# Products for relative values over two tokens each, with near probabilities stored by pairs and four narrower transposes

## The reference

```python
B, T, C = x.shape                     # 8, 512, 128; H = 16 heads, d = 8
q, k, v = split(layernorm(x) @ w_attn)            # each (B, H, T, d)
rel = jnp.tril(idx[:, None] - idx[None, :])       # 0..511, clipped by indexing to 0..127
rk, rv = embk[rel], embv[rel]
att = jnp.einsum('bhtd,bhsd->bhts', q, k) * scale + jnp.einsum('bhtd,tsd->bhts', q, rk)
att = softmax(where(causal, att, -inf))
y = jnp.einsum('bhts,bhsd->bhtd', att, v) + jnp.einsum('bhts,tsd->bhtd', att, rv)
x = x + y.reshape(B, T, C) @ w_proj
x = x + experts(layernorm(x))
```

## Time and profile before

| | before |
|---|---|
| median of 3 runs | 797.58 us (796.44 to 797.76) |
| profiled execution, own time | 790.65 us |
| its span | 788.9 us |
| TensorE matmul busy | 705.4 us (89%) |
| VectorE busy | 588.3 us (75%) |
| ScalarE busy | 516.9 us (66%) |
| GpSimd busy | 255.8 us (32%) |

### The profile page before, as it was taken

The page is one execution under the profiler, slowest core; times in us unless marked ns, Lnnn a source line. Parts: engine busy times, 40 slices in busy tenths (PEclk is TensorE's granted clock), DMA queues, the critical chain, the costliest instruction groups (busy, mean ns, idle before and its releaser), DMA issues. The chain is left out here.

```text
span 788.9 us, 27137 instructions
## 1 busy us (share of the span) xinstructions
PE 705.4 (89%) x10368; PEld 511.1 (65%) x10368; DVE 588.3 (75%) x2036; ACT 516.9 (66%) x1032; POOL 255.8 (32%) x253
## 2 busy tenths in 40 slices
PE   3757779996989998988998988997999999999998
PEld 1545547775767677766777766775566666666665
DVE  6855667885878788888888878887367776776676
ACT  2576777885888777898887898877424434443331
POOL 9343355432545533445633535533000000000000
PEclk9897999998999999999999999999799999999999
DMA  9699999988688878778778678851000000000000
GB/s 305 230 277 287 329 271 291 299 268 253 220 250 264 292 229 249 239 217 268 232 230 253 211 239 252 260 160 47 2 22 27 27 1 27 28 15 0 14 15 14
DMA packets 116687, 140.32 MB, mean 178 GB/s; under 512 B 8848, under 2 KB 83088, under 8 KB 116368
## 3 DMA queue, kind: packets, MB, share of 16 engines
q1 hardware_dynamic: 116560, 138.59, 57.5%
HBM read 82.26 MB, written 56.30 MB: 176 GB/s over the span
## 5 line engine op out<-in xcount | busy, mean ns | idle before, releaser
L1041 DVE CUSTOM_DVE_ANT_0 ps<-ps,near 128x128 f32<-128x128 f32 (+3 forms) x512 | 244.8, 509 | 94.7 <-PE ps L812 63.1
L966 ACT ACTIVATE work<-ps,nmin 128x128 f32<-128x128 f32 (+3 forms) x512 | 249.8, 545 | 72.4 <-DVE nmin L1041 65.4
L824 PE MATMUL ps<-ident,work 128*128 128x128 f32 x1280 | 204.9, 280 | 13.9 <-issue 12.7
L824 PEld LDWEIGHTS ps<-ident,work 128*128 128x128 f32 x1280 | 159.0, 144 | 36.8 <-issue 18.9
L812 PE MATMUL ps<-kb,qb 128*128 128x128 bf16 (+3 forms) x512 | 131.5, 309 | 19.8 <-ACT work L966 15.9
L770 POOL TENSOR_SCALAR_AFFINE_SELECT work<-work 128x512 f32<-128x512 f32 x96 | 61.3, 638 | 242.2 <-ACT work L955 201.9
L1358 ACT ACTIVATE near<-ps 128x512 f32<-128x512 f32 x80 | 47.6, 595 | 136.6 <-PE ps L1323 136.5
L774 POOL TENSOR_TENSOR work<-work 128x512 f32<-128x512 f32 x96 | 124.3, 1295 | 8.0
L1026 DVE COPY work<-ps 128x512 f32<-128x512 f32 (+1 forms) x192 | 123.1, 641 | 1.0 <-PE ps L824 1.0
L1333 PEld LDWEIGHTS ps<-work,near 128*128 128x128 f32 x640 | 82.5, 191 | 34.3 <-issue 31.7
L841 PE MATMUL ps<-work,vb 128*9 128x128 f32 x2560 | 96.7, 279 | 0.8 <-ACT relS L944 0.8
(11 more groups left out here) (110 smaller groups left out, 629.6 us busy)
## 6 DMA issues: line engine op xcount, KB each, us to landing
near<-w_slots SPq DMA_DIRECT2D x96, 512.0 KB, 5.3
w_slots<-relS SPq DMA_DIRECT2D x128, 256.0 KB, 4.7
qk_rows<-work SPq DMA_DIRECT2D x36, 256.0 KB, 4.2
near<-w_slots SPq DMA_DIRECT2D x32, 256.0 KB, 4.6
w_slots<-near SPq DMA_DIRECT2D x8, 512.0 KB, 6.0
qk_rows<-y SPq DMA_DIRECT2D x9, 256.0 KB, 5.5
qb<-qk_rows SPq DMA_DIRECT2D x24, 96.0 KB
kb<-qk_rows SPq DMA_DIRECT2D x24, 96.0 KB
```

The costliest lines, as they stand in the source:

```text
L824: ins = nc.tensor.transpose(tp_ps[:, m % 2, n * P:(n + 1) * P], prob[:, m % PROBS, n * P:(n + 1) * P], ident[:, :])
L966: ins = nc.scalar.activation(prob[:, m % PROBS, h * wide:(h + 1) * wide], qk_ps[:, m % 3, h * wide:(h + 1) * wide], ACT.Exp, bias=nmin[:, ...
L1041: nc.vector.tensor_tensor_reduce(out=scores, in0=scores, in1=near[:, q % NEAR, a, 4 * P - wide:4 * P, r], scale=1.0, scalar=3e38, op0=ALU. ...
```

## The change

A product for relative values now covers two tokens, k and 64 + k. pcT is stored by pairs: for each k first the 32 heads of token k, then those of token 64 + k, so one product has 64 columns of weights. Its data are the 16 columns of both tokens in tv, which the host now orders by pairs. The output is 64 partitions x 16 columns, of which the two quarters that combine one token's probabilities with the other token's values are not used. The outputs of k = 0 to 31 lie at partitions 0 to 63 and those of k = 32 to 63 at partitions 64 to 127; the bank is filled over all its 512 columns. There are 64 products in an e, 8 in a chunk.

near_values(e, side) turns half of the bank with two transposes, each from 32 partitions of PSUM (one token of each pair) to the 32 partitions of rvn that hold these tokens. Side 0 runs where the single transpose ran, side 1 a slot later; for the last e both run in the same step. rvn_done now counts four for every e, and whoever waited for e + 1 waits for 4 (e + 1). GpSimd's instructions are the same in number, with the token dimension split in two.

```diff
@@ -553,7 +553,7 @@
         prob = prob.rearrange("p (n t) -> p n t", t=T)
         pT = pT.rearrange("p (k h t) -> p k h t", k=2, h=4)
         ptmp = ptmp.rearrange("p (h t) -> p h t", h=4)
-        pcT = pcT.rearrange("p (k t n) -> p k t n", k=2, t=P)
+        pcT = pcT.rearrange("p (k t n) -> p k t n", k=2, t=P // 2)
         rvn = rvn.rearrange("p (n d) -> p n d", d=D)
         ysum = ysum.rearrange("p (b h d) -> p b h d", b=2, d=D)
         yn = yn.rearrange("p (b c) -> p b c", b=GB)
@@ -609,7 +609,7 @@
         READ = {
             "rel": lambda q: (rel_done, q + 1),
             "av": lambda n: (av_copied, n + 1),
-            "rv": lambda e: (rvn_done, e + 1),
+            "rv": lambda e: (rvn_done, 4 * (e + 1)),
             "yt": lambda e, b: (ysum_done, GB * e + b + 1),
             "yb": lambda e: (ynT_done, e + 1),
             "pj": lambda e: (x1_done, e + 1),
@@ -761,9 +761,10 @@
                     wait_copied(pool, last(q))
                     if u == 0 and e >= 2:
                         pool.wait_ge(rv_ready, RVN * (e - 1))
-                    dst = pcT[:, e % 2, :, 4 * u:4 * u + 4].rearrange("p t h -> p h t")
+                    dst = pcT[:, e % 2, :, :].rearrange("p k (j n) -> p n j k", j=2)[:, 4 * u:4 * u + 4]
+                    by_pair = lambda v: v.rearrange("p h (j k) -> p h j k", j=2)
                     if i == 0:
-                        nc.gpsimd.tensor_copy(dst, pT[:, q % 2, :, 0:P]).then_inc(pc_done, 1)
+                        nc.gpsimd.tensor_copy(dst, by_pair(pT[:, q % 2, :, 0:P])).then_inc(pc_done, 1)
                         return
                     near_q = sum(row(k) > 0 for k in range(q))
                     wait(pool, pc_done, q)
@@ -771,7 +772,7 @@
                                             compare_op=ALU.is_gt, fill=0.0, base=0, pattern=[[0, 4], [-1, P]],
                                             channel_multiplier=1).then_inc(ptmp_done, 1)
                     pool.wait_ge(ptmp_done, near_q + 1)
-                    nc.gpsimd.tensor_tensor(dst, ptmp[:, :, :], pT[:, q % 2, :, i * P:(i + 1) * P],
+                    nc.gpsimd.tensor_tensor(dst, by_pair(ptmp[:, :, :]), by_pair(pT[:, q % 2, :, i * P:(i + 1) * P]),
                                             ALU.add).then_inc(pc_done, 1)
 
                 first["pool"](pool)
@@ -852,10 +853,10 @@
                     bank = misc("rv", e)
                     lot = 32 // RVN
                     for a in range(lot * c, lot * (c + 1)):
-                        for tq in range(4):
-                            tau = 32 * tq + a
-                            ins = nc.tensor.matmul(bank[32 * tq:32 * tq + NH, a * D:(a + 1) * D], pcT[:, e % 2, tau, :],
-                                                   tv[:, tau, :], start=True, stop=True)
+                        for side in range(2):
+                            k = 32 * side + a
+                            ins = nc.tensor.matmul(bank[64 * side:64 * side + 2 * NH, a * 2 * D:(a + 1) * 2 * D],
+                                                   pcT[:, e % 2, k, :], tv[:, 2 * k:2 * k + 2, :], start=True, stop=True)
                     ins.then_inc(rv_ready, 1)
 
                 def yt(e, b):
@@ -1042,20 +1043,24 @@
                                                        scale=1.0, scalar=3e38, op0=ALU.add, op1=ALU.min,
                                                        accum_out=nmin[:, k % MINS:k % MINS + 1]).then_inc(min_done, 1)
 
-                def near_values(e):
+                def near_values(e, side):
                     dve.wait_ge(rv_ready, RVN * (e + 1))
                     wait(dve, ysum_done, GB * e)
                     if e == 0:
                         dve.wait_ge(*first["third_rows"])
-                    nc.vector.transpose(rvn[:, :, :].rearrange("p n d -> p d n"),
-                                        misc("rv", e)[:, 0:32 * D].rearrange("p (t d) -> p d t", d=D)).then_inc(rvn_done, 1)
+                    for j in range(2):
+                        lot = slice(64 * side + 32 * j, 64 * side + 32 * j + 32)
+                        tokens = slice(64 * j + 32 * side, 64 * j + 32 * side + 32)
+                        nc.vector.transpose(rvn[tokens, :, :].rearrange("p n d -> p d n"),
+                                            misc("rv", e)[lot, :].rearrange("p (t j d) -> p j d t", j=2, d=D)[:, j]
+                                            ).then_inc(rvn_done, 1)
 
                 def normalise(e, b):
                     n = GB * e + b
                     dve.wait_ge(yt_ready, n + 1)
                     turned = misc("yt", e, b).rearrange("p (u q r) -> p u q r", u=4, r=32)
                     nc.vector.reciprocal(rden[:, b, :, :], turned[:, :, :, D]).then_inc(rden_done, 1)
-                    dve.wait_ge(rvn_done, e + 1)
+                    dve.wait_ge(rvn_done, 4 * (e + 1))
                     nc.vector.tensor_tensor(ysum[:, b, :, :].rearrange("p (u q) d -> p u q d", u=4),
                                             turned[:, :, :, 0:D],
                                             rvn[:, H * b:H * (b + 1), :].rearrange("p (u q) d -> p u q d", u=4),
@@ -1083,9 +1088,12 @@
                         pT_copy(m - 4)
                     if m < NU:
                         scores_min(m)
+                    for kind, *what in OPS[m - 2] if m > 1 else []:
+                        if kind == "rv" and what[1] == RVN - 1:
+                            near_values(what[0], 1)
                     for kind, *what in OPS[m - 1] if m else []:
                         if kind == "rv" and what[1] == RVN - 1:
-                            near_values(what[0])
+                            near_values(what[0], 0)
                         if kind == "yt":
                             normalise(*what)
                         if kind == "pj":
@@ -1096,7 +1104,8 @@
                 def last_row(step):
 
                     if step == 1:
-                        near_values(GI - 1)
+                        near_values(GI - 1, 0)
+                        near_values(GI - 1, 1)
                     if step in (2, 3):
                         normalise(GI - 1, step - 2)
                     if step == 6:
@@ -1466,7 +1475,8 @@
     heads = [4 * u + 2 * side + j for side in range(2) for u in range(H // 4) for j in range(2)]
     by_dim = np.arange(C).reshape(H, D)[heads].T.reshape(C)
     columns = np.concatenate([by_dim, C + by_dim, 2 * C + np.arange(C)])
-    turn = (np.arange(NREL)[None, :] - np.arange(P)[:, None]) % NREL
+    token = np.arange(P).reshape(2, P // 2).T.reshape(P)
+    turn = (token[None, :] - np.arange(P)[:, None]) % NREL
     def twice(rows):
         placed = np.zeros((P, rows.shape[1]), np.float32)
         for at, first_row, n in sum(PLACES, []):
```

## The result

| | kernel before | changed kernel |
|---|---|---|
| median | 797.53 us | 847.47 us |
| lowest and highest of 4 | 796.44, 797.76 | 844.38, 850.88 |
| profiled execution | 790.65 us, span 788.9 | 848.96 us, span 847.2 |
| mean granted clock | 0.970 | 0.931 |

Forecast was 833.9 us, range 808 to 852: direction and range hold, and the loss is 50 us where the sum said 36.3.

A forecast was written before the change was run, and what follows sets the result against it. TensorE was taken to set the pace, with VectorE following. Terms 25.3 + 1.4 + 15 + 2.6 - 3 - 5 = +36.3 us on a median of 797.58 gave 833.9 us, range 808 to 852.

The forecast's parts named there:

- The product's length: Line 857 on TensorE: loading 64 columns instead of 32 adds 0.21 us a chunk, +25.3 us over 120 chunks.
- Rival 4: TensorE's products: a record costs a fixed time whatever its columns, so the kernel gets faster, -8.3 us, 789.3; chance 0.06.
- rival 3: TensorE's products: two groups of 64 load as fast as four of 32 did, +9.4 us, 807.0; chance 0.06.
- The switch of width: TensorE from line 841 to 857: groups of 32 then 64 columns cost 0.11 us at 12 chunks, +1.4 us.
- Record stalls: Two unexplained mid-chunk stalls on TensorE, 4.1 us together, may be spared by half the records: -3 us.
- Absorbed: Until 190 us transfers limit, so part of the added length of row blocks 0 to 2 goes into stops: -5 us.
- The transposes: VectorE: four transposes for one add 1.97 us a row block; half reaches TensorE, +15 us over 15 row blocks.
- Rival 2: VectorE's added transposes show in full, 29.6 us, and the bank's wait adds 8: +64 us, 861.7; chance 0.07.
- Rival 1: VectorE's added transposes are hidden by its idle sixth and the longer slots: +20.4 us, 818.0; chance 0.15.
- GpSimd at nothing: GpSimd's near probabilities, written with a wider stride, may take longer, but its idle time covers it: 0 us.
- The last row block: Head of the expert part: longer products add 1.7 us on TensorE, transposes arrive 1.1 late; together +2.6 us.

The follow-up runs named there:

- swapped: Changed products with one transpose on 128 partitions, operands exchanged (16 columns of weights, 64 of data), against the kernel before: 797.27 us, ratio 1.0029.
- swapped4: Changed kernel, all four transposes kept, with the products' operands exchanged (16 columns of weights, 64 of data), against the kernel before: 819.35 us, ratio 1.0371.
- moved64: Changed kernel with 64 columns of data per product instead of 16, still 64 columns of weights, against the kernel before: 829.59 us, ratio 1.0385.
- Narrow: Changed products cut to 32 columns of weights, 16 of data, with one transpose on 128 partitions, against the kernel before: 783.96 us, ratio 0.9873.
- products: Changed products, but one transpose on 128 partitions instead of four on 32, against the kernel before: 807.66 us, ratio 1.0199.

## Why the prediction was right and wrong

In parts, each ratio turned into us of 797.5: the products with their stretch taken off are +3.5 to +6 (15.9 less the 9 to 10 of the stretch; or swapped's 2.3 plus 120 x 0.01 = 1.2 for its shorter slots). The transposes are +24. The half clock is +20 to +26 (changed less swapped4 is 20.7, less 1.2 for shorter slots; changed less moved64 is 19.6, plus 6 for longer ones). Together 47 to 56, measured 50; each ratio is known to within 3 to 8 us, so the parts are too.

- **The product's length: right.** Load 138 ns against 139, a chunk 0.65 us as forecast, a slot +0.20 against +0.21 (0.17 of it in the chunk, 0.03 before the scores that follow it). Narrow and products differ in the columns loaded alone and by 0.187 us a chunk at the same record count. Rival 4 (a price for each record, 789.3) and rival 3 (64 load like 32, 807.0) fall. Beside rival 4 stood the Trainium skill, page "TensorEngine Tiling (Array Packing)", section "Instruction Overhead", with some 60 cycles for each matmul (25 ns at 2.4 GHz, an estimate from that page's figure). As a price for every record it fails where groups stand side by side: 32 records in 0.263 us (before) are 8 ns each. Taken for each group by itself it is not contradicted: a round takes 31 to 33 ns in narrow and before, but 0.058 us once 64 columns are loaded.
- **The switch of width: right.** Between lines 842 and 858 loading now stops for 0.22 us where it followed without idle time. Start to start it is 0.20 against 0.09 at full clock, the 0.11 that was counted:

```profile
253.21 0.12 PEld L842 LDWEIGHTS ps<-work,vb 128*9 128x9 f32 x8 [0.17 <-issue]
253.54 0.55 PEld L858 LDWEIGHTS ps<-tv,work 128*64 128x64 f32 x16 [0.22 <-issue]
```

- **Record stalls: right in kind, mis-sized.** -3 was taken from the two stalls of the earlier trace rows; there are ten of over 0.15 us at line 857, 9.1 us of its 9.6 us of idle time, and all are gone. Narrow, with before's chunk length and half the records, is 10 us faster. Two stalls had been read, not their number; the row of groups of the kernel before gives it at its end:

```profile
L857 PE MATMUL ps<-tv,work 128*32 128x8 f32 x4096 | 58.8, 179 | 9.6 <-issue 9.1
```

- **Absorbed: -5 forecast, 12 to 14 by the runs.** 24 (120 slots by 0.20) + 1.3 + 1.5 - 9 = 18, and only 3.5 to 6 arrive. In the changed kernel VectorE's stops for transfers shrink, from 108 to 590 us, before and then changed:

```profile
DVE ps L1041 <- DMA near<-w_slots: 15.8, 15, 4.6
DVE work L1074 <- DMA xr<-in_x: 3.3, 3, 1.7
```

```profile
DVE ps L1042 <- DMA near<-w_slots: 9.1, 11, 2.0
```

  With the products alone they are 16.8 and 1.5, hardly less than before, so they are not where the products' 12 to 14 us went; that is mostly open. In row block 10 of the products run one slot gives back 0.97 us, where VectorE waited for the residual's rows before. What was absorbed isn't bound to the first 190 us, as the prediction had it: row blocks 6, 10 and 14 give theirs back too (41.4, 41.0 and 32.1 us before, 41.5, 41.5 and 32.3 with the products alone, where 8 chunks should add 1.6).
- **The transposes: the failed step is "of 1.97 us I let half through".** Their length was right (0.646 against 0.66, 64 times), the sum of +15 was not: +24. VectorE's sixth of idle time doesn't lie where it is needed. In the row block above no idle time of VectorE stands between the minimum at 295.56 and the copy at 299.71, and behind two pairs TensorE stops within one slot. Rival 2 had the better mechanism (nearly all arrives, and the bank's wait is there, some 6 us in place of 8) but added the two to 37.6 us, further from 24 than the forecast's 15. Rival 1 falls.
- **The half clock: missing in the prediction, rivals included.** 20 to 26 us. The earlier trace rows gave the price of a half-clock stretch, and nothing asked whether the new products could lengthen one.
- **GpSimd at nothing, right** (1290 ns against 1295). **The last row block:** its two lots take 2.04 us each against 1.31, +1.5 for the 1.7 counted, and its transposes 2.67 us; what of it arrived wasn't separated.

That the total fell into the range was luck: the products' part came 14 to 17 us lower than forecast (20.4 without the transposes, measured 3.5 to 6), the transposes' 9 higher, and the clock's 20 or more, which nothing in the prediction counted, were added.

## What to carry to other kernels

Price a small matmul by the columns that it loads or moves, whichever are more, not by its count: joining two tokens in one product halved the count and the useful share, and saved only the stalls between records. Price an added instruction on an engine that feeds the bounding one nearly in full when it stands in one place of the order, whatever that engine's mean idle share (here 24 of 29.6 us). Look at the granted clock by stretches for every new shape on TensorE: here the same products with four times the data columns were 20 us faster than the changed form. None of the variants that compute the reference beat the kernel before.

## What the hardware did that wasn't expected

- During a stop of 0.9 to 2.3 us, or at most 2.1 us behind it, TensorE's granted clock fell to 0.50 and stayed there for 17 to 34 us, with TensorE busy for 96% of it or more, only with products of 64 columns loaded and 16 moved. With 64 loaded and 64 moved, 16 and 64, 32 and 16, or 32 and 8, no stretch was longer than 10.2 us in the attention (13.7 with the products in two lots). Why the one shape holds it down is open.
- A 32x32-block transpose on VectorE takes 0.646 us for 32 partitions and 0.658 for 128, with 256 elements along each.
- Records of 8 columns, 59 in 1.02 us, run into gaps of 0.5 to 5.7 us, each ending 2.2 to 3.3 us behind the start of a packet of instructions; in the seven kernels with half as many there was none in the attention.
- With two groups side by side a round goes by the larger of what it loads and moves: a chunk of 8 rounds takes 0.249 us with 32 columns loaded and 16 moved, 0.436 with 64 and 16, 0.408 with 16 and 64, 0.463 with 64 and 64.
- 64 columns of data in place of 16 behind a load of 64 add 0.027 us to a chunk of 8 rounds, 3 ns a round: they pass almost wholly beside the load.
